# Reordering the start of a tile, and moving the place where TensorE's loop body ends, in a fused attention and FFN kernel

## The chip, the cores and the metric

One core of one Trainium2 chip. The time is device microseconds of one execution of the whole program. Median, lowest and highest are those of the runs shown; one further execution was recorded by the hardware profiler, and every row below comes from it.

## What is computed

A transformer layer over x of 4096 rows and 512 columns, float32, without a batch dimension to speak of:

```python
qkv = x @ w_qkv.T                       # 16 heads of 32, q, k, v
q, k = rope(q), rope(k)
scores = q @ k.T * scale                # a row sees itself and the 63 rows before it
out = softmax(scores) @ v @ w_out.T
x = layernorm(x + out)
gate = silu((x @ w_gate) * s_gate)      # 512 to 2048, int8 weights
up = (x @ w_up) * s_up
x = layernorm(x + ((gate * up) @ w_down) * s_down)
```

## The kernel before, in words

The rows are cut into 8 tiles of 512 (TILE), each of 4 blocks of 128 (NB = 4). Attention of tile a runs together with the FFN of tile a - 1: the 16 steps of a tile (STEPS) hold one gate product and one up product of the FFN each, and between them one group of four heads of one block of attention: scores, maxima, exponentials, weights (probabilities), their transpose by DMA, and the product with the values (weigh_v). Values and projections are float32; numbers that go into a float16 product are split into a high and a low half (split_high on ScalarE, split_low on GpSimd, split_v and split_x1 on VectorE).

Each engine has its program written out by hand, in order, with semaphores between them; nothing is planned by a tool. Each program has a first part, then a loop (Fori) over tiles whose body is back(t) followed by front(t + 1), then the last tiles. Tile 1 has a front of its own (is_early); the front that the diff touches runs for tiles 2 to 7.

- **TensorE** (from line 1035). back ends with project_pair (queries and keys) and begin_values. front begins with project_values: two row pairs (i = 0, 1), each of seven products of 128x256 called first, fifth, sixth, third, seventh, second, fourth (the values are made with seven products instead of eight, so several write one place of a bank one after the other, and each such product waits until ScalarE has copied the one before out, keep_values_...). Among them stand scores(0) and scores(1). Then the steps: gate s, up s, and after odd steps two weigh_v and two scores. weigh_v(0) and weigh_v(1) stand behind up 3, scores(5) and scores(6) behind them. The front ends with the output projection and the down blocks 0 and 1; back begins with spread_maximum (a small product that spreads the next tile's largest input) and the down blocks 2 and 3. So the loop body of TensorE ends between down blocks 1 and 2.
- **ScalarE** (from line 1506). Copies of the products, split_high(2) and split_high(3) (four parts each: two of the queries, two of the keys, of blocks 2 and 3), exponentials(0), keep_v (high half of the values), exponentials(1), then per step a tanh, copies and exponentials.
- **VectorE** (from line 2093). add_v (finishes the values of a block), maxima and bias of a group, weights, split_v; then per step two operations of swiglu, maxima, bias, weights. GpSimd's and VectorE's sums of a tile's inputs lie in ffn_tmp and probs, where later the FFN's and attention's values go.
- **GpSimd** (split_low, line 797). split_low(1), (2), (3) in this order, four subtractions each (L800), every one behind the part of split_high that it needs; then per step split_probs (L690) and split_fuse (L695).
- **SyncE**, which issues the DMAs in order. turn_qk(0), (1), (2) transpose queries and keys of a block and each wait until split_low of that block is done (qk_low); behind them cross_v(0), cross_v(1) (four DMAs L571), turn_probs(0) (a transpose, L587), cross_v(2), turn_probs(1), cross_v(3), and so on. weigh_v(1) waits for turn_probs(1) to have landed. The order is:

```python
for j in range(1, NB - 1):
    turn_qk(a, j)
for j in range(2):
    cross_v(a, j)
for s in range(STEPS):
    turn_probs(a, s, ffn)
    if s < 2:
        cross_v(a, NB - 2 + s)
```

## Time and profile before

| | |
|---|---|
| runs: median, lowest, highest | 1166.68 us, 1164.76, 1167.25 |
| profiled execution, its own time | 1166.12 us |
| its span, first to last instruction | 1164.3 us |
| TensorE busy | 1148.5 us, 99% |
| VectorE, ScalarE, GpSimd busy | 84%, 53%, 52% |
| granted TensorE clock | 0.998 of full speed |

The time of the profiled execution is its span and 1.8 us around it. Busy is the share of the span in which the engine had an instruction under way; the ends of matmuls are modelled, so two that follow each other without a stall overlap in the rows, and the distance from start to start tells more than the duration.

### The profile page before, as it was taken

The numbers are of one execution on the slowest core, as the hardware profiler recorded it, in microseconds if no ns is written. First come the engines' busy times: TensorE is split into PE (matmuls) and PEld (weight loads), VectorE is DVE, ScalarE is ACT, GpSimd is POOL, SyncE is SP. The second block draws the span as 40 slices with busy tenths as digits, with TensorE's granted clock in tenths as the row PEclk, the third lists the DMA queues.
The fourth block names the chain that finished last, engine by engine and source line by source line (L and its number), as shares of the span: only waits on it lengthen the run. The fifth ranks groups of instructions, "written<-read, shape, count | busy, mean of one in ns | idle before, by whom it ended". The sixth has DMA issues, their size and how long they took to land.

```text
span 1164.3 us, 25889 instructions
## 1 busy us (share of the span) xinstructions
PE 1148.5 (99%) x8577; PEld 595.0 (51%) x8577; DVE 976.0 (84%) x2797; ACT 622.3 (53%) x1724; POOL 600.5 (52%) x570
## 2 busy tenths in 40 slices
PE   9999999999999999999999999999999999999998
PEld 4344446464464644646455464554645545464444
DVE  7889998889997899878999789887898978986434
ACT  3863883159920689117980279702796038950330
POOL 0775684356731667326771367614676245752330
PEclk9999999999999999999999999999999999999999
DMA  9999786357672585717757077561874627644000
GB/s 295 161 186 242 140 172 147 85 100 139 121 174 56 96 139 112 175 40 124 138 98 166 37 142 127 97 160 38 151 123 91 166 58 136 126 74 109 19 1 37
DMA packets 353042, 139.59 MB, mean 120 GB/s; under 512 B 309968, under 2 KB 332624, under 8 KB 352912
## 3 DMA queue, kind: packets, MB, share of 16 engines
q1 hardware_dynamic: 334976, 106.86, 49.6%
q0 software_dynamic: 10800, 18.09, 5.3%
q10 hardware_dynamic: 7136, 12.93, 3.2%
q8 instruction: 78, 1.28, 0.5%
q14 instruction: 52, 0.43, 0.1%
HBM read 36.13 MB, written 9.18 MB: 39 GB/s over the span
## 4 chain that ended last, share of the span: by engine, by line
PE 78%; DVE 7%; issue 6%; POOL 3%; DMA 3%; ACT 2%; SPq 1%; ACTq 0%; DVEq 0%; POOLq 0%
PE bank L906 52%; PE bank L1217 17%; PE bank L916 3%; PE bank L1143 2%; DMA xT_sb<-xT_sb 2%; DVE v_own L1794 2%; POOL xT_sb L690 1%; ACT bank L1457 1%; PE bank L1123 1%; ACT fuse L1356 1%; POOL fuse L695 1%; DVE ffn_tmp L1844 1%; DMA qkT<-fuse 1%; DVE bank L1831 1%; DVE probs L1809 1%
## 5 line engine op out<-in xcount | busy, mean ns | idle before, releaser
L906 PE MATMUL bank<-x1T,wg 128*128 128x512 f16 (+1 forms) x1032 | 242.5, 378 | 1.1 <-DVE ffn_tmp L1844 1.1
L906 PE MATMUL bank<-x1T,wu 128*128 128x512 f16 x1024 | 241.9, 379 | 0.0
L1457 ACT ACTIVATE bank<-bank,neg_max,qk_scale 128x128 f32<-128x128 f32 x512 | 220.4, 434 | 23.5 <-DVE neg_max L1837 22.4
L1217 PE MATMUL bank<-wd,fuse 128*128 128x512 f16 (+2 forms) x1056 | 223.3, 373 | 0.7 <-DVE y L1892 0.6
L695 POOL TENSOR_TENSOR fuse<-ffn_tmp,fuse 128x512 f16<-128x512 f32 x128 | 149.7, 1170 | 96.5 <-ACT fuse L1356 96.2
L800 POOL TENSOR_TENSOR fuse<-fuse 128x512 f16<-128x512 f32 x116 | 142.6, 1266 | 88.3 <-ACT fuse L1356 86.1
L1217 PEld LDWEIGHTS bank<-wd,fuse 128*128 128x128 f16 x1056 | 101.6, 98 | 118.7 <-DVE y L1892 1.6
L906 PEld LDWEIGHTS bank<-x1T,wu 128*128 128x128 f16 x1024 | 100.2, 98 | 120.6
L690 POOL TENSOR_TENSOR xT_sb<-probs,xT_sb 128x512 f16<-128x512 f32 x112 | 131.0, 1170 | 52.2 <-ACT xT_sb L1356 52.0
L906 PEld LDWEIGHTS bank<-x1T,wg 128*128 128x128 f16 x1032 | 96.4, 98 | 112.7 <-DVE ffn_tmp L1844 2.0
L1366 ACT ACTIVATE ffn_tmp<-bank,tanh_scale 128x512 f32<-128x512 f32 x128 | 88.7, 693 | 65.9 <-PE bank L906 42.2
L1831 DVE CUSTOM_DVE_ANT_0 bank<-bank,mask_tile 128x128 f32<-128x128 f32 x448 | 116.3, 321 | 7.6 <-issue 7.6
L1848 DVE SCALAR_TENSOR_TENSOR ffn_tmp<-bank,fuse_scale,ffn_tmp 128x512 f32<-128x512 f32 x128 | 96.1, 751 | 18.8 <-PE bank L906 6.6
L1844 DVE SCALAR_TENSOR_TENSOR ffn_tmp<-ffn_tmp,bank 128x512 f32<-128x512 f32 x128 | 86.8, 678 | 25.6 <-ACT ffn_tmp L1366 25.5
L1457 ACT ACTIVATION_READ_ACCUMULATOR bank<-bank,neg_max,qk_scale 128x1 f32 x512 | 105.6, 206 | 0.0
L885 POOL TENSOR_TENSOR rstd<-mean_var,half_power 128x1 f32<-128x1 f32 x32 | 24.0, 751 | 144.1 <-DVE mean_var L1865 138.6
L1356 ACT ACTIVATE fuse<-bank 128x512 f32<-128x512 f32 x24 | 14.3, 597 | 140.7 <-PE bank L906 138.8
L1356 ACT ACTIVATE fuse<-ffn_tmp 128x512 f16<-128x512 f32 x128 | 80.7, 630 | 16.1 <-DVE ffn_tmp L1848 16.1
L1809 DVE SCALAR_TENSOR_TENSOR probs<-bank,inv_sum 128x512 f32<-128x512 f32 x120 | 82.9, 691 | 4.8 <-DVE inv_sum L1804 0.3
L1356 ACT ACTIVATE fuse<-fuse 128x512 f16<-128x512 f32 x120 | 65.5, 619 | 36.4 <-DVE fuse L1635 36.4
L1627 DVE TENSOR_TENSOR fuse<-bank,tables 128x512 f32<-128x512 f32 x120 | 75.5, 681 | 3.8 <-POOL fuse L800 3.1
L815 POOL TENSOR_TENSOR rstd<-mean_var,half_power 128x1 f32<-128x1 f32 x32 | 23.8, 745 | 98.4 <-DVE mean_var L1865 98.4
(258 smaller groups left out, 1846.7 us busy)
## 6 DMA issues: line engine op xcount, KB each, us to landing
v_cross<-v_own SPq DMA_DIRECT2D x64, 128.0 KB, 2.4
out<-x ACTq DMA_DIRECT2D x31, 256.0 KB, 2.0
xT_sb<-xT SPq DMA_DIRECT2D x30, 256.0 KB, 4.9
qkT<-x SPq DMA_DIRECT2D x28, 256.0 KB, 3.2
wg<-w_gate POOLq DMA_DIRECT2D x7, 1024.0 KB, 5.7
v_cross<-kept_v_weights ACTq DMA_DIRECT2D x5, 768.0 KB, 7.5
wu<-w_up POOLq DMA_DIRECT2D x7, 512.0 KB, 6.3
wqkv<-w_qkvT SPq DMA_DIRECT2D x8, 256.0 KB, 6.2
```

The lines of the kernel that those rows point to most:

```text
L690: done(probs_low, pool.tensor_tensor(place[:, 1, :, :], probs_place(s, ffn), place[:, 0, :, :], ALU.subtract))
L695: done(fuse_low, pool.tensor_tensor(fuse[:, s, 1, :], ffn_tmp[:, s % 2, :], fuse[:, s, 0, :], ALU.subtract))
L800: last = pool.tensor_tensor(*low_operands(j, i, ffn), ALU.subtract)
L906: last = pe.matmul(dst, lhsT, rhs, start=(i == 0 and not onto), stop=(i == len(pairs) - 1), skip_group_check=onto)
L1217: last = pe.matmul(dst[:, cols], fuse[:, s, z, rows], wd[:, s, cols], start=(s == 0 and z == 0), stop=(s == STEPS - 1 and z == 1))
L1356: return act.activation(dst, src, ACT.Copy, scale=scale)
L1366: done(tanh_done, act.activation(ffn_tmp[:, s % 2, :], bank32[2 * (s % 2)], ACT.Tanh, scale=tanh_scale[:, s:s + 1]))
L1457: last = act.activation(unit, unit, ACT.Exp, bias=neg_max[:, s % 2, h // 3, h % 3:h % 3 + 1], scale=qk_scale[:, 2:3], accum_out=row_sum[:, ...
L1809: done(probs_ready, dve.scalar_tensor_tensor(out=probs_place(s, ffn), in0=units, scalar=2.0 ** PROB_BITS, in1=inverse, op0=ALU.mult, op1=A ...
L1831: last = dve.tensor_tensor_reduce(out=unit, in0=unit, in1=mask_tile[:, :], scale=1.0, scalar=MASKED, op0=ALU.add, op1=ALU.max, accum_out=r ...
L1844: done(gated, dve.scalar_tensor_tensor(out=tmp, in0=tmp, scalar=1.0, in1=bank32[2 * (s % 2)], op0=ALU.add, op1=ALU.mult))
L1848: done(fused, dve.scalar_tensor_tensor(out=tmp, in0=bank32[2 * (s % 2) + 1], scalar=fuse_scale[:, s:s + 1], in1=tmp, op0=ALU.mult, op1=ALU ...
```

## The change

The order on three engines changes at the start of the fronts of tiles 2 to 7. On TensorE the second product of pair 0 comes earlier, and scores(0) and scores(1) come before sixth, fourth, third and seventh of what is left. On ScalarE the key half of split_high(2) and all of split_high(3) move behind copies and exponentials. On VectorE maxima and bias of groups 0 and 1 come before add_v(1), and the split_v are spread between others, with one more wait: weights(0) overwrites probs, which seventh(1) reads. The programs of GpSimd and SyncE are as before. Apart from that, TensorE's loop body ends behind down block 2 instead of behind down block 1; the order of its products there stays down 0, down 1, spread_maximum, down 2, down 3.

```diff
-        V_FIRST, V_FIFTH, V_SIXTH, V_THIRD, V_SEVENTH, V_SECOND, V_FOURTH = range(7)
+        V_FIRST, V_FIFTH, V_SIXTH, V_THIRD, V_FOURTH = 0, 1, 2, 3, 6
+        V_SECOND, V_SEVENTH = (4, 5), (5, 4)
...
             def project_values(a):
                 values_sixth(a, 0)
                 values_third(a, 0)
+                values_second(a, 0)
                 values_fifth(a, 1)
                 values_seventh(a, 0)
+                scores(a, 0, True)
+                scores(a, 1, True)
                 values_sixth(a, 1)
-                values_second(a, 0)
                 values_fourth(a, 0)
                 values_third(a, 1)
                 values_seventh(a, 1)
-                scores(a, 0, True)
-                scores(a, 1, True)
                 values_second(a, 1)
                 values_fourth(a, 1)
...
-                for j in range(2):
+                for j in range(NB - 1):
                     down(f, j, attn)
+                    if more and j == 1:
+                        spread_maximum(a)
 
             def back(t, more, attn=True):
                 a, f = t, t - 1
-                if more:
-                    spread_maximum(a)
-                for j in range(2, NB):
-                    down(f, j, attn)
+                down(f, NB - 1, attn)
...
                     keep_values_sixth(a, 0)
                     keep_values_fifth(a, 1)
                     keep_values_seventh(a, 0)
+                    split_high(a, 2, ffn, range(2))
                     keep_values_sixth(a, 1)
-                    split_high(a, 2, ffn)
+                    exponentials(a, 0, ffn)
                     keep_values_seventh(a, 1)
-                    split_high(a, 3, ffn)
-                    exponentials(a, 0, ffn)
                     keep_v(a, 0, ffn)
                     keep_v(a, 1, ffn)
+                    split_high(a, 2, ffn, range(2, 4))
                     exponentials(a, 1, ffn)
+                    split_high(a, 3, ffn)
                     keep_v(a, 2, ffn)
                     keep_v(a, NB - 1, ffn)
...
                     add_v(a, 0)
-                    add_v(a, 1)
                     for s in range(2):
                         maxima(a, s, ffn)
                         bias(a, s)
-                        add_v(a, 2 + s)
+                    add_v(a, 1)
+                    wait(v_product[1], dve, a - 2, V_SEVENTH[1])
                     weights(a, 0, ffn)
-                    for j in range(2):
-                        split_v(a, j, ffn)
+                    add_v(a, 2)
+                    split_v(a, 0, ffn)
+                    add_v(a, NB - 1)
+                    split_v(a, 1, ffn)
                     weights(a, 1, ffn)
                     for j in range(2, NB):
                         split_v(a, j, ffn)
```

## Rows read from the trace of the kernel before

**Rows 1.** The page, busy time of each engine

```profile
PE 1148.5 (99%) x8577; PEld 595.0 (51%) x8577; DVE 976.0 (84%) x2797; ACT 622.3 (53%) x1724; POOL 600.5 (52%) x570
```

**Rows 2.** TensorE's waits from 200 us on: total, times, longest

```profile
PE bank L1143 <- DMA xT_sb<-xT_sb: 2.0, 4, 0.6
PE bank L906 <- DVE ffn_tmp L1844: 1.1, 6, 0.2
PE bank L1196 <- issue: 0.8, 1, 0.8
PE bank L1217 <- DVE y L1892: 0.6, 1, 0.6
```

**Rows 3.** Timeline of TensorE in tile 3: start, duration, instructions

```profile
400.78 0.52 PE L1123 MATMUL bank<-qkT 128*32 128x96 f16 x32
401.23 1.13 PE L906 MATMUL bank<-wqkv,xT_sb 128*128 128x256 f32 x4
...
411.14 1.90 PE L906 MATMUL bank<-x1T,wg 128*128 128x512 f16 x8 [0.17 <-DVE ffn_tmp L1844]
...
418.39 0.28 PE L1143 MATMUL bank<-xT_sb,v_cross 128*32 128x128 f16 x8
...
418.61 0.84 PE L1123 MATMUL bank<-qkT 128*32 128x96 f16 x32
419.38 1.90 PE L906 MATMUL bank<-x1T,wg 128*128 128x512 f16 x8
```

**Rows 4.** Timeline of ScalarE at the start of tile 3

```profile
397.80 2.18 ACT L1356 ACTIVATE fuse<-fuse 128x512 f16<-128x512 f32 x4
400.88 0.47 ACT L1356 ACTIVATE v_cross<-bank,v_scale 128x256 f32<-128x256 f32 x1 [0.90 <-PE bank L906]
...
408.90 0.71 ACT L1366 ACTIVATE ffn_tmp<-bank,tanh_scale 128x512 f32<-128x512 f32 x1
```

**Rows 5.** The page, costliest groups: one exponential

```profile
L1457 ACT ACTIVATE bank<-bank,neg_max,qk_scale 128x128 f32<-128x128 f32 x512 | 220.4, 434 | 23.5 <-DVE neg_max L1837 22.4
```

**Rows 6.** Timeline of GpSimd, split_low(2) and (3) of tile 3

```profile
398.50 9.43 POOL L800 TENSOR_TENSOR fuse<-fuse 128x512 f16<-128x512 f32 x8 [6.81 <-ACT fuse L1356]
```

**Rows 7.** Instructions of line 800, tile 3: duration ns min, median, max

```profile
L800 POOL TENSOR_TENSOR fuse<-fuse x8: 1156/1161/1610, 398.5 to 406.3; 128x512 f16<-128x512 f32 x8
```

**Rows 8.** Timeline of VectorE in tile 3

```profile
406.84 1.64 DVE L1794 TENSOR_TENSOR v_own<-ffn_tmp,v_own 128x512 f16<-128x512 f32 x1
...
410.41 0.68 DVE L1844 SCALAR_TENSOR_TENSOR ffn_tmp<-ffn_tmp,bank 128x512 f32<-128x512 f32 x1
```

**Rows 9.** Timeline of SyncE's issues in tile 3

```profile
403.12 4.55 SPq L541 DMA_TRANSPOSE qkT<-fuse  x2
...
407.95 2.52 SPq L571 DMA_DIRECT2D v_cross<-v_own  x4
...
411.61 2.03 SPq L587 DMA_TRANSPOSE xT_sb<-xT_sb  x1
...
415.25 1.24 SPq L587 DMA_TRANSPOSE xT_sb<-xT_sb  x1
```

**Rows 10.** Timeline of SyncE's issues in tile 1

```profile
126.11 2.51 SPq L571 DMA_DIRECT2D v_cross<-v_own  x4
...
131.63 1.25 SPq L587 DMA_TRANSPOSE xT_sb<-xT_sb  x1
```

**Rows 11.** Timeline of TensorE in tile 7, the weigh_v behind step 3

```profile
987.29 0.30 PE L1143 MATMUL bank<-xT_sb,v_cross 128*32 128x128 f16 x8 [0.45 <-DMA xT_sb<-xT_sb]
```

**Rows 12.** Timeline of TensorE at a loop end

```profile
635.29 0.23 PE L1196 MATMUL bank<-unit_rows,next_max 128*128 128x128 bf16 x1
```

**Rows 13.** Windows before the old and the new loop end: busy, clock, DMA share, GB/s

```profile
348.40:352.00 3.60, 3.60 (x19) 1.57 (x17) 3.37 (x6) 0.63 (x1) 0.00 (x0) 1.00 0.59 113
355.30:358.90 3.60, 3.60 (x19) 1.60 (x18) 3.29 (x16) 0.00 (x0) 0.00 (x0) 1.00 0.02 5
```

**Rows 14.** Timeline of GpSimd before a late loop end

```profile
772.27 0.74 POOL L794 DMA_DIRECT2D wu<-w_up  x1 [6.88 <-issue]
```

More of the change, by code:

```diff
@@ L1408, in keep_values_seventh @@
             def keep_values_seventh(a, i):
-                keep_value_product(a, i, v_rows(2 * i + 1)[:, 0:HALF_EMB], v_places(i)[3], V_SEVENTH)
+                keep_value_product(a, i, v_rows(2 * i + 1)[:, 0:HALF_EMB], v_places(i)[3], V_SEVENTH[i])
             def carry_v(a):
@@ L1786, in add_v @@
                 wait(v_products_kept[i], dve, a - 2, 2 + back)
-                wait(v_product[i], dve, a - 2, V_FOURTH if back else V_SECOND)
+                wait(v_product[i], dve, a - 2, V_FOURTH if back else V_SECOND[i])
                 done(v_added, dve.scalar_tensor_tensor(out=v_rows(j), in0=bank32[j], scalar=v_scale[:, 1:2],
```

## The prediction

> **What bounds the kernel.** I read the page first: TensorE is busy for 1148.5 of the 1164.3 us [rows 1], so the change can win only stalls of TensorE, and anything it adds to TensorE's path is paid in full. Next come TensorE's waits from 200 us on, behind the odd first tiles: four kinds, 4.5 us together [rows 2]. Two belong to the front and its consequences: the third gate product waits for VectorE's first swiglu operation in each of the six tiles, and four weigh_v wait for a transposed block of probabilities. The view leaves out the start-up of a stall: the 32 score matmuls take 0.45 us from start to start where nothing waits (400.78 to 401.23), 0.77 us behind weigh_v(1) in tile 3 (418.61 to 419.38) [rows 3], where scores(6) waits for weights(3) of VectorE. Last I read the queues that feed weigh_v(1): ScalarE to GpSimd (L800) to SyncE to the DMA. There the point of the change lies. In tile 3 turn_probs(1) is issued at 415.25 [rows 9] and weigh_v(1) starts at 418.39 [rows 3], without a wait: at most 3.14 us from issue to use. In tile 7 the same product already waits 0.45 us [rows 11]. So there is next to no slack on this path.
>
> **TensorE's values and scores.** The same products in another order; nothing is added, and the number of changes between scores and values is the same. In tile 3, scores(0) and (1) move from 400.78 by four 128x256 products of about 0.86 us to about 397.3, sixth(1) to 397.8, seventh(1) to 400.5, and the first gate product stays where it is. ScalarE's copy of seventh(1) began 1.07 us behind its product's start, so it moves from 400.88 [rows 4] to about 401.54 and lasts 0.47; fourth(1), which waits for it, still begins at 402.2. Slack 0.2 us: cost nothing, at worst 0.1 us per tile.
>
> **ScalarE.** The same work again. The query half of split_high(2) starts at 397.80 as before; copies of 128x512 follow each other in 0.52 us (2.18 us for four) [rows 4]. Then sixth(1) is copied at 398.95 to 399.3, exponentials(0) take 4 x 0.434 = 1.74 us [rows 5] to 401.1, the engine idles to 401.54 for seventh(1), then keep_v(0) and (1) to 402.95. Only then come the two key parts of split_high(2), 402.95 to 404.0, exponentials(1) to 405.7, split_high(3) to 407.8, two keep_v to 408.85, and the first tanh: 408.85 against 408.90 before [rows 4]. ScalarE gains nothing for the FFN; VectorE does, for split_v(2) and (3) now lie right behind the copies instead of behind weights(1): its first swiglu operation moves from 410.41 [rows 8] to about 409.65. A lead of 0.75 us takes away the wait of the third gate product and of scores(6). The added wait of weights(0) for seventh(1), done at 401.5, holds VectorE's add_v(2) and split_v(0) for 0.4 us, in time that it had to spare before exponentials(1).
>
> **GpSimd and SyncE, whose programs do not change.** This is the cost. Before, split_low(2) began at 398.50, 0.70 us behind its first part [rows 4, 6], and eight subtractions took 9.43 us with one of 1.61: the seven others 1.12 apart, so the fourth ended at 402.97 and SyncE issued the transposes of block 2 at 403.12 [rows 6, 7, 9]. Now its third part can start at 402.95 + 0.70 = 403.65 and the fourth ends at 405.9: 2.9 us later. SyncE works in order, and behind that pair stand cross_v(0) and (1), turn_probs(0), cross_v(2), turn_probs(1). From the pair's issue to the first cross_v it takes 4.83 us [rows 9]; from there to turn_probs(1), when nothing but SyncE itself is waited for, 5.52 us (tile 1, 126.11 to 131.63) [rows 10]. That gives 403.12 + 2.9 + 4.83 + 5.52 = 416.4 instead of 415.25, and weigh_v(1) at 416.4 + 3.1 = 419.5 instead of 418.39: **1.1 us more** per tile. The slack between cross_v and turn_probs(0) (1.1 us idle, and the latter's 2.03 us against 1.24) [rows 9] is already used up in this sum. Split_low(3) ends near 408.1 + 3.1 = 411.2, still ahead of turn_probs(0), which SyncE now reaches at 413.6.
>
> **A collision that may lengthen it.** One split_v lasted 1.64 us beside L800 instead of 0.68, and one L800 1.61 instead of 1.16 [rows 7, 8]. In the new order split_v(0) and (1) fall on the two key parts. Bounds: nothing, or 0.45 us more per tile; no row decides, and I take the middle, 0.2. The Trainium skill (SBUF — State Buffer, in its text on the shared port pair) says that a VectorE operation with two SBUF inputs and a GpSimd operation that reads SBUF exclude each other for the whole instruction. By that rule the upper end would hold and the total below would be 1.5 us higher; the trace agrees as far as the lengths of these two instructions go.
>
> **The sum over six tiles.** Tiles 2 to 6 lose 1.3 us each, tile 7, which waits 0.45 us there already (0.6 with the stall's start-up), about 0.7: +7.2. Behind this stall TensorE is about 1 us later, so other stalls vanish: scores(6) in five tiles, 0.32 us each less what one of them lacks, -1.5; the weigh_v of step 7 in three tiles, 2.0 - 0.45 = 1.55 us [rows 2, 11] with 0.17 us start-up for each, -2.1. The wait of the third gate product goes too, but it lies ahead of weigh_v(1), which starts at an absolute time: it brings nothing. Total of the front: **+3.6 us**.
>
> **The loop end.** spread_maximum began at 635.29 [rows 12], 0.26 us late behind a loop end; at another end the wait was 0.8 us with nothing in the profile that ended it [rows 2], but there the next product had to wait for VectorE anyway. DMA engines are 0.59 busy in the stretch ahead of the old end and 0.02 in that 7 us later [rows 13]. I take -0.3 us; the bounds are 0 and -1.1. The page Runtime: NRT & Kernel Launch of the Trainium skill (Instruction fetch mechanics) says a taken branch breaks the sequential prefetch and makes the target be fetched by a DMA. By it a quiet DMA stretch shortens the branch, which supports the -0.3; if the fetch has a fixed cost instead, the sum would be 0.3 higher.
>
> Against the profiled execution's own 1166.12 us this makes 1166.12 + 3.6 - 0.3 = **1169.4 us**; that execution lies 0.6 us below the median of the runs shown, within their spread.
>
> **Rivals.**
> - *Slower as worked out*, 1167 to 1172: 46 in 100. For it: SyncE's order, and a stall that tile 7 already shows.
> - *Faster, because SyncE's chain is not the last* (26). It decides if turn_probs(1) is issued by 415.25 despite the push, that is if the key parts come no more than 1.8 us later (1.1 idle and 0.75 in turn_probs(0)'s longer issue), or if the pair of transposes is issued 1 us faster. Then weigh_v(1) follows the earlier weights, and all stalls go: six gate waits of 0.24 = 1.4, scores 1.5, step 7 2.1, tile 7 0.6, loop 0.3: 5.9 us, 1160.2. Half of it is 1163. Against it: 2.9 us is fixed by seventh(1) and two copies.
> - *No change* (18): the stall is 1.1 us or less and the one stray event of the old trace, a GpSimd DMA issue held for 6.88 us [rows 14] that made that tile about 2 us longer, does not come back: 1166.12 + 2 - 2 = 1166.
> - *Slower by more* (10): turn_probs(0) or (1) keeps an issue of 2.03 us although SyncE comes straight from cross_v: +0.75 us per tile, 1174; both, 1178.
>
> **Numbers.** About 0.2% (2.3 us) is what a measurement of this kernel can tell from no change, so slower starts at 1169.0. The main case spreads over that line: of its 46 some 8 fall within 0.2%, the last rival adds 10 to slower: 0.48. The range has to take in half and most of the faster case and one slow issue per tile: 1161.5 to 1175.
>
> **What would show it.** Right: L541 for block 2 issued about 3 us later after the first gate product; SyncE going from cross_v straight to turn_probs(0) and (1); a wait of about 1 us of L1143 for a DMA behind step 3 in each of tiles 2 to 7; no wait of L906 for L1844. Wrong: turn_probs(1) issued at the old distance from the first gate product; L1143 waits as few as before; new waits of the values' fourth product for ScalarE; a longer spread_maximum gap at the new loop end.

## The result, and the profile after

The changed kernel takes **1186.32 us** (median; 1183.64 to 1188.15), beside 1165.92 us (1164.76 to 1167.25) for the kernel before on the same chip: a ratio of 1.0173, with a 95% interval of 1.0149 to 1.0196. It is slower, as forecast, but by 20 us and not by 3. The profiled execution took 1185.87 us with a span of 1184.0 us, 19.75 us more than the one shown of before, and it is this difference that is taken apart here.

The page of the changed kernel, busy time of each engine (of before: [rows 1]):

```profile
PE 1150.9 (97%) x8577; PEld 595.2 (50%) x8577; DVE 981.1 (83%) x2797; ACT 622.9 (53%) x1724; POOL 604.8 (51%) x570
```

The same 8577 matmuls are busy for 2.4 us more (some ran at a lower clock, below), while the span grew by 19.7. The time is in stalls. TensorE's waits in the changed kernel from 200 us on (total, times, longest):

```profile
PE bank L1144 <- DMA xT_sb<-xT_sb: 11.2, 7, 2.3
PE bank L1218 <- issue: 7.6, 4, 2.3
PE bank L907 <- DVE ffn_tmp L1845: 3.1, 6, 0.5
```

Against [rows 2]: the wait of weigh_v for a transposed block grew from 2.0 to 11.2 us, the wait of the third gate product from 1.1 to 3.1 us instead of going away, and a kind that was not there stands at the down products (L1218), four times, with nothing in the profile that ends it. Measured from start to start of the matmuls, which takes in the start-up of each stall, the difference is: loop ends +9.7 us, weigh_v(1) +11.6, third gate product +2.0, and -3.5 for stalls of scores(6) and of step 7's weigh_v that went. That is 19.8 of the 19.75 us.

**The front.** TensorE in tile 3, timeline of the changed kernel (start, duration, instructions, idle time before and what ended it; lines are one further down than in [rows 3]):

```profile
408.89 1.89 PE L907 MATMUL bank<-x1T,wg 128*128 128x512 f16 x8
...
417.32 1.90 PE L907 MATMUL bank<-x1T,wg 128*128 128x512 f16 x8 [0.51 <-DVE ffn_tmp L1845]
...
426.39 0.29 PE L1144 MATMUL bank<-xT_sb,v_cross 128*32 128x128 f16 x8 [1.65 <-DMA xT_sb<-xT_sb]
```

From here on G is the start of the first gate product of a tile: 403.06 us in tile 3 before, 408.89 after. weigh_v(1)'s waiting product starts at G + 17.50 instead of G + 15.33. Behind it stand the queues. ScalarE in the same tile, timeline of the changed kernel (of before: [rows 4]):

```profile
408.78 1.14 ACT L1356 ACTIVATE fuse<-fuse 128x512 f16<-128x512 f32 x2
...
414.68 0.69 ACT L1366 ACTIVATE ffn_tmp<-bank,tanh_scale 128x512 f32<-128x512 f32 x1
```

GpSimd in the same tile and view (of before: [rows 6]):

```profile
404.33 2.28 POOL L801 TENSOR_TENSOR fuse<-fuse 128x512 f16<-128x512 f32 x2 [6.81 <-ACT fuse L1356]
409.47 8.21 POOL L801 TENSOR_TENSOR fuse<-fuse 128x512 f16<-128x512 f32 x6 [2.87 <-ACT fuse L1356]
```

SyncE's issues, likewise (of before: [rows 9]):

```profile
412.31 4.66 SPq L542 DMA_TRANSPOSE qkT<-fuse  x2
417.25 2.85 SPq L572 DMA_DIRECT2D v_cross<-v_own  x4
420.44 1.24 SPq L588 DMA_TRANSPOSE xT_sb<-xT_sb  x1
...
423.28 1.23 SPq L588 DMA_TRANSPOSE xT_sb<-xT_sb  x1
```

ScalarE splits the keys at 408.78. GpSimd, which before did eight subtractions in a row, does two, stands still for 2.87 us, and does six; the fourth ends at 412.2. SyncE issues the pair of transposes at G + 3.42 (before G + 0.06), and from there to turn_probs(1) at G + 14.39 (before G + 12.19) its issues follow each other almost without a pause. The block lands 3.1 us later, and weigh_v(1) starts.

VectorE in tile 3, timeline of the changed kernel (of before: [rows 8]):

```profile
414.30 0.80 DVE L1795 TENSOR_TENSOR v_own<-y,v_own 128x512 f16<-128x512 f32 x1 [1.69 <-ACT v_own L1356]
415.02 1.65 DVE L1795 TENSOR_TENSOR v_own<-v_cross,v_own 128x512 f16<-128x512 f32 x1
416.58 0.68 DVE L1845 SCALAR_TENSOR_TENSOR ffn_tmp<-ffn_tmp,bank 128x512 f32<-128x512 f32 x1
```

VectorE has been idle for 1.69 us, and then split_v(3) lasts 1.65 us, beside GpSimd's subtractions. The first swiglu operation starts at G + 7.69 instead of G + 7.35: later, not earlier.

**The loop end.** TensorE's timeline around the second loop end of the changed kernel (of before: [rows 12]):

```profile
503.82 5.29 PE L1218 MATMUL bank<-wd,fuse 128*128 128x512 f16 x23
511.15 5.10 PE L1218 MATMUL bank<-wd,fuse 128*128 128x512 f16 x15 [2.05 <-issue]
```

The window behind the stall (busy time of PE, PEld, DVE, ACT, POOL, then granted clock, DMA share, GB/s, as in [rows 13]):

```profile
511.20:514.60 3.40, 3.40 (x9) 1.24 (x10) 0.62 (x3) 0.00 (x0) 1.34 (x2) 0.52 0.24 84
```

In the middle of a run of the same kind a down product starts late: at 364.31, 511.15, 658.00 and 802.88 us, by 2.50, 2.21, 1.69 and 1.80 us. That is once per round of the loop, each time behind the fourth product of the new body. Behind the first two of these stalls the clock granted to TensorE is about half (0.52 in this window, so 1.2 instead of 2.4 GHz for nearly all of its 3.4 us), after TensorE had stood still for over 2 us; 7 or 8 products then take 0.43 us each in place of 0.216, 1.7 us more.

### The profile page after: what moved, and what is told of

It is laid out like the page before. It is cut to its first block, busy times and chain, and to the rows that moved or that the text cites. A ratio compares the mean times of both kernels' runs of the same rounds, so it can differ in the third digit from the quotient of the medians.

```text
span 1184.0 us, 25906 instructions
## 1 busy us (share of the span) xinstructions
PE 1150.9 (97%) x8577; PEld 595.2 (50%) x8577; DVE 981.1 (83%) x2797; ACT 622.9 (53%) x1724; POOL 604.8 (51%) x570
## 4 chain that ended last, share of the span: by engine, by line
PE 70%; issue 11%; POOL 6%; SPq 5%; DVE 4%; DMA 3%; ACT 1%; POOLq 0%; ACTq 0%; DVEq 0%
PE bank L907 43%; PE bank L1218 18%; POOL fuse L801 5%; PE bank L1144 3%; SPq L542 2%; DMA xT_sb<-xT_sb 2%; SPq L572 2%; PE bank L917 2%; PE bank L1124 1%; PE bank L933 1%; DVE fuse L1628 1%; DMA out<-x 1%; SPq L588 1%; PE bank L1240 1%; ACT bank L1457 1%
## 5 line engine op out<-in xcount | busy, mean ns | idle before, releaser
L1218 PE MATMUL bank<-wd,fuse 128*128 128x512 f16 (+2 forms) x1056 | 227.1, 376 | 7.6 <-issue 7.6
L801 POOL TENSOR_TENSOR fuse<-fuse 128x512 f16<-128x512 f32 x116 | 148.6, 1310 | 105.9 <-ACT fuse L1356 103.5
L1218 PEld LDWEIGHTS bank<-wd,fuse 128*128 128x128 f16 x1056 | 102.1, 99 | 129.7 <-issue 15.1
L886 POOL TENSOR_TENSOR rstd<-mean_var,half_power 128x1 f32<-128x1 f32 x32 | 24.0, 750 | 154.6 <-DVE mean_var L1866 149.1
L1356 ACT ACTIVATE xT_sb<-probs 128x512 f16<-128x512 f32 x112 | 70.6, 631 | 8.2 <-DMA xT_sb<-xT_sb 8.1
```

The source lines that it names most:

```text
L801: last = pool.tensor_tensor(*low_operands(j, i, ffn), ALU.subtract)
L1218: last = pe.matmul(dst[:, cols], fuse[:, s, z, rows], wd[:, s, cols], start=(s == 0 and z == 0), stop=(s == STEPS - 1 and z == 1))
L1356: return act.activation(dst, src, ACT.Copy, scale=scale)
```

## The experiments

Fifteen kernels in four groups, each group on one chip beside the kernel before.

**First group: which half of the change costs what, and is it the place of the loop body?** TensorE's whole instruction stream was counted in the built programs: ahead of the loop's body stand 3447 instructions in the kernel before and 3514 in the changed one (a float16 product counts as 2, its weight load and itself; a float32 product as 4). The bodies are equally long. The traces agree: 2224 instructions stand between two branches in every kernel, and 67 more ahead of the first branch in the changed one. Theory A: a position of the body's start is bad, whatever the order of the work. Theory B: the new loop end itself is bad.

loop_alone is the kernel before with the change's loop end:

```diff
-                for j in range(2):
+                for j in range(NB - 1):
                     down(f, j, attn)
+                    if more and j == 1:
+                        spread_maximum(a)
```

> The kernel before with TensorE's loop end behind down block 2 and nothing else. Theory: the loop end costs by itself, and the front has no part in it. Adding up the stalls of TensorE in the two traces, the four loop ends cost about 12 us in the changed kernel and 2 in the one before, so I expect +8 to +10 us against before (about 1175), a stall of 1.7 to 2.5 us a few products behind each of four loop ends, and the granted clock at half behind some of them. Rival: the stall comes from TensorE being late through the new front; then this kernel is within 2 us of before.

Measured: 1176.71 us (1175.85 to 1180.75) beside 1165.59, ratio 1.0109 [1.0086, 1.0132]. The one kind of its waits that grew beyond a microsecond or so, in that view (L1143's wait for a DMA went from 2.0 to 3.3 us):

```profile
PE bank L1217 <- issue: 8.4, 4, 2.3
```

The loop end alone brings the four stalls and costs 11 us, one more than the 8 to 10 expected.

front_alone is the changed kernel with the old loop end (the diff above, reversed).

> The changed kernel with TensorE's loop end back behind down block 1. Theory: the front costs what the delayed chain through SyncE costs: +10 us against before (about 1176), with weigh_v(1) waiting 1.6 to 2.2 us for its transposed block in each of tiles 2 to 7, no stall at loop ends over 0.5 us, and the clock at full speed. Rival (front and loop end act together): the sum of this kernel's and loop_alone's differences is more than 3 us away from the 20 us of the whole change.

Measured: 1176.15 us (1175.62 to 1176.59), ratio 1.0093 [1.0076, 1.011]. Its waits:

```profile
PE bank L1144 <- DMA xT_sb<-xT_sb: 11.4, 7, 2.2
PE bank L907 <- DVE ffn_tmp L1846: 3.1, 6, 0.5
PE bank L1197 <- issue: 1.6, 2, 1.1
```

The front alone costs 10.6 us, and 11.1 + 10.6 = 21.7 is within 1.3 us of the 20.4 us of both: the two halves very nearly add. One part of the expectation missed: with the old loop end a wait for issue of 1.1 us stands at spread_maximum (L1197), where none over 0.5 was expected. This is the small stall of [rows 2] (0.8 us at L1196) again; more on it below.

The other two shift the body by waits that have long been met, at each step of TensorE's first down blocks, ahead of the loop. new_end_shifted has the new loop end and two such waits per step of block 0, which the built program has as one instruction, 16 in all: its body starts at 3530. old_end_shifted has the old loop end and five per step of blocks 0 and 1, 68 instructions: 3515.

```diff
+                        if isinstance(f, int) and f == 0 and j in (0,):
+                            for _ in range(2):
+                                pe.wait_ge(wd_in, 4 * 16)
                         for z in range(2):
```

> The kernel before, loop end where it was, but 68 instructions (waits that are met at once) put into TensorE's program ahead of the loop, in the first down blocks, so that the loop body begins at the same place of the instruction stream, to one instruction, as in the changed kernel. Theory A, what counts is where the body's first instruction lies in the stream: stalls of about 2 us a few products behind each loop end, +8 to +10 us against before. Theory B, what counts is which products stand behind the loop end or what the DMA engines do at that time: within 1 us of before, no stall over 0.5 us.

> loop_alone, with 16 instructions (waits that are met at once) put into TensorE's program ahead of the loop, so that the body begins 16 instructions later in the stream than in the changed kernel. In its trace the stall came about 10 instructions behind the body's first. Theory A, place in the stream: the stall is gone, the time is that of before within 1.5 us. Theory B, the place of the loop end among the products: as loop_alone, +8 to +10 us.

Measured: old_end_shifted 1179.34 us (1177.34 to 1181.23), ratio 1.0114 [1.0092, 1.0136]; new_end_shifted 1162.15 us (1161.13 to 1163.38), ratio **0.9972 [0.9961, 0.9983]**. TensorE's waits for issue in old_end_shifted, in the same view as above:

```profile
PE bank L1220 <- issue: 12.0, 4, 3.1
PE bank L1196 <- issue: 1.7, 3, 1.1
```

(Three lines of 0.2 to 1.1 us are left out.) Its timeline behind a loop end, with spread_maximum and one down product of the new body done:

```profile
500.85 15.21 PE L1220 MATMUL bank<-wd,fuse 128*128 128x512 f16 x63 [2.94 <-issue]
```

And the waits of new_end_shifted (one line more, of 0.3 us, is left out):

```profile
PE bank L906 <- DVE ffn_tmp L1846: 1.1, 6, 0.2
PE bank L1143 <- DMA xT_sb<-xT_sb: 0.6, 1, 0.6
```

That settles A against B. The old loop end, moved to where the change had put the body, stalls as the new one does; the new one, 16 instructions further on, has no wait for issue in the view, and the kernel is 3.4 us faster than before. Both sizes missed, though not the side: old_end_shifted costs 13.8 us instead of 8 to 10, for its four stalls are longer (3.0 to 3.3 us), and new_end_shifted was expected within 1.5 us of before.

**Second group: the front.** Theory Q is the prediction's: the late key parts hold turn_qk(2), and SyncE hands the delay on, in order. Theory G: VectorE and GpSimd are late with the probabilities themselves. All four start from front_alone or from one another. keys_ahead lets ScalarE split all of block 2 early; sync_reordered leaves ScalarE alone and moves one issue of SyncE:

```diff
-                    split_high(a, 2, ffn, range(2))
+                    split_high(a, 2, ffn)
                     keep_values_sixth(a, 1)
...
-                    split_high(a, 2, ffn, range(2, 4))
```

The edit of sync_reordered, in SyncE's program:

```diff
-                    for j in range(1, NB - 1):
-                        turn_qk(a, j)
+                    turn_qk(a, 1)
                     for j in range(2):
                         cross_v(a, j)
+                    turn_qk(a, 2)
```

> This kernel has the new front and the old loop end (as front_alone, 1176.15 us, where TensorE waited 11.4 us in 7 stalls of 2.2 us for the second half of the transposed probabilities at L1144), and ScalarE makes all four high parts of score block 2 before it keeps the sixth products of the second half. Theory Q (the weigh_v wait is handed on through SyncE's fixed order: the late low part of block 2 holds turn_qk(2), and turn_qk(2) holds everything SyncE issues behind it): GpSimd's low parts of block 2 end about as early as in the kernel before, turn_qk(2) is issued at the first gate product of the tile instead of 3.4 us behind it, and the wait at the second weigh_v falls from 2.2 us to about 0.5 us a tile. ScalarE keeps the sixth and the seventh products about 0.5 us later, for which TensorE should wait at values_fourth(1), some 0.35 us a tile. In all 6 to 8 us less than front_alone: 1168 to 1170 us. Theory G (the probabilities are late because VectorE's and GpSimd's own work on them is late, and SyncE's order has nothing to do with it): the wait at the second weigh_v stays at 2 us or more, and the time stays at 1175 to 1178 us.

> This kernel is front_alone (1176.15 us) with one issue of SyncE moved: turn_qk(2) is issued behind cross_v(0) and cross_v(1) instead of ahead of them. No engine's own work is touched. Theory Q: cross_v(0) is no longer held until 3.4 us behind the first gate product, turn_probs(0) follows as soon as GpSimd's probabilities of block 0 are there (9.9 us behind the first gate product instead of 11.5), turn_probs(1) at about 12.5 instead of 14.4, and the second weigh_v waits 0.2 to 0.5 us a tile instead of 2.2: about 10 us less than front_alone, 1165 to 1167 us. The wait of the third gate product (0.58 us in six tiles) stays. Theory G: turn_probs(1) is issued when VectorE and GpSimd are done with block 1, which this edit doesn't change: 1175 to 1178 us. A third outcome: turn_qk(2) is now late for whoever reads the turned keys of block 2; then a new wait stands at the scores of block 2.

Measured: keys_ahead 1166.9 us (1164.37 to 1168.45), ratio 1.0005 [0.9995, 1.0015]; sync_reordered 1170.51 us (1169.38 to 1170.9), ratio 1.0036 [1.0021, 1.005]. The waits of keys_ahead from 200 us on (one more, for issue at L1197, 1.2 us in two, is left out):

```profile
PE bank L1144 <- DMA xT_sb<-xT_sb: 2.8, 7, 0.6
```

SyncE's issues in tile 3 of keys_ahead, G = 406.56:

```profile
406.18 4.53 SPq L542 DMA_TRANSPOSE qkT<-fuse  x2
...
415.57 1.94 SPq L588 DMA_TRANSPOSE xT_sb<-xT_sb  x1
...
419.11 1.24 SPq L588 DMA_TRANSPOSE xT_sb<-xT_sb  x1
```

The waits of sync_reordered (left out again: for issue at L1197, 0.9 us):

```profile
PE bank L1144 <- DMA xT_sb<-xT_sb: 5.5, 10, 1.1
PE bank L907 <- DVE ffn_tmp L1846: 3.1, 6, 0.5
```

SyncE's issues in tile 3 of sync_reordered, G = 405.15:

```profile
405.91 2.67 SPq L572 DMA_DIRECT2D v_cross<-v_own  x4
409.00 4.38 SPq L542 DMA_TRANSPOSE qkT<-fuse  x2
415.16 1.84 SPq L588 DMA_TRANSPOSE xT_sb<-xT_sb  x1
...
418.60 1.23 SPq L588 DMA_TRANSPOSE xT_sb<-xT_sb  x1
```

Q holds. With the keys early, turn_qk(2) is issued at G - 0.38 and turn_probs(1) at G + 12.55, close to the G + 12.19 of before. With only SyncE's order changed and every engine's own work as in front_alone, turn_probs(1) comes at G + 13.45 in place of 14.39, and the kernel wins 5.6 us. It was forecast to win 10: turn_probs(0) came at G + 10.0 as expected, but turn_probs(1) was 0.9 us later than the 12.5 expected. That turn_probs(0) was 1.84 us under issue and not 1.24 makes 0.6 of it, and half of the wait at L1144 stayed (5.5 of 11.4 us). In keys_ahead the feared wait for ScalarE's copies did not come, and the gate products' waits for VectorE went altogether (its first swiglu operation started at 413.25, G + 6.69), which was not forecast: it is about what it won beyond the 6 to 8 us (9.3 us).

values_later is sync_reordered with two splits of VectorE moved, and both_mended adds to it the new loop end and 16 instructions, start at 3530:

```diff
                     weights(a, 1, ffn)
-                    for j in range(2, NB):
-                        split_v(a, j, ffn)
...
+                    if s == 1 and attn and not is_early(a):
+                        for j in range(2, NB):
+                            split_v(a, j, ffn)
```

> This kernel is sync_reordered with VectorE's splits of the last two value blocks moved behind its first swiglu. Theory V (the wait of the third gate product is VectorE's first swiglu, which ends later because the splits ahead of it run beside GpSimd's work at 1.60 to 1.65 us in place of 1.16 or 0.80): the first swiglu starts at least 1.5 us earlier than 7.7 us behind the first gate product, and the 6 waits of 0.5 us at the third gate product go: about 3 us less than sync_reordered, 1162 to 1164 us. Rival: that wait isn't VectorE's but ScalarE's tanh (5.8 us behind the first gate product in both kernels); then the six waits stay and the time is that of sync_reordered. What can go wrong: the last two blocks of split values come later for cross_v(2) and cross_v(3), and the third weigh_v waits instead.

> This kernel is values_later with the new loop end, and with 16 instructions more on TensorE ahead of the loop, so that the body of the loop starts 3530 instructions into TensorE's stream, where the kernel with the new loop end alone and shifted so (1162.15 us, ratio 0.9972) had no stall behind its four loop branches. Theory A (the stall behind a loop branch comes of where the body lies in the stream, not of the new loop end): no stall over 0.3 us behind any of the four branches, the granted clock stays at full speed, and the gain of the mended front adds to that of the shifted end: 1157 to 1161 us, faster than the kernel before. Rival: the new loop end leaves too little queued work when the front's waits are gone, and the four stalls of 1.7 to 2.5 us are back with about 10 us: 1170 us.

Measured: values_later 1178.57 us (1177.83 to 1179.57), ratio 1.0108 [1.0091, 1.0125]; both_mended 1176.94 us (1176.61 to 1177.51), ratio 1.0097 [1.008, 1.0114]. Both expectations missed. The waits of values_later that grew:

```profile
PE bank L907 <- DVE ffn_tmp L1846: 9.5, 6, 1.6
PE bank L1124 <- DVE probs L1811: 5.2, 6, 0.9
```

VectorE in tile 3 of values_later, G = 405.80, timeline:

```profile
413.78 1.58 DVE L1796 TENSOR_TENSOR v_own<-y,v_own 128x512 f16<-128x512 f32 x1
415.29 1.64 DVE L1796 TENSOR_TENSOR v_own<-v_cross,v_own 128x512 f16<-128x512 f32 x1
...
418.12 0.68 DVE L1846 SCALAR_TENSOR_TENSOR ffn_tmp<-ffn_tmp,bank 128x512 f32<-128x512 f32 x1
```

Of theory V the direction holds: the first swiglu operation came at G + 6.5 (412.31), 1.2 us sooner, and the third gate product no longer waited. But now both splits ran at 1.58 and 1.64 us, in front of the maxima and the second swiglu operation, and the fourth gate product waited 1.6 us, the scores 0.9. The 3.1 us of splits only changed the product that waits for them. both_mended has no wait for issue at its loop ends (its view has none, and from start to start no product behind a branch is more than 0.23 us late), so the part of its expectation on them holds; the rest fell with values_later.

**Third group: the position again, and a best version.** after_shifted is the changed kernel itself plus the 16 instructions (3530). new_end_later is the kernel before with the new loop end and 256 of them, 16 at each step (3770, which is 3514 + 256).

> This is the changed kernel itself (1186.32 us) with 16 waits more, already met, in TensorE's instructions ahead of the loop, so that the loop's body starts 3530 instructions into its stream instead of 3514. The work and its order are those of the changed kernel. Theory A (where the body lies decides the stall behind the branch): the four stalls of 1.7 to 2.5 us and the half clock behind two of them go, a round of the loop falls from 144.5 to 147.5 us to about 143 us, and the time is that of the new front alone, 1174 to 1177 us. Rival B (the new loop end leaves too little queued work at the branch once the new front changes what comes ahead of it): the stalls stay, 1184 to 1188 us.

> This is the kernel before with the new loop end, as in new_end_shifted (1162.15 us), but with 256 met waits ahead of the loop instead of 16: the body starts 3770 instructions into the stream, 256 behind the 3514 at which loop_alone stalled (1176.71 us, rounds of 145.5, 143.7 and 144.1 us against 141.0 us with the body at 3530). Theory A in its sharper form (instructions come in blocks of 256, and it is the place within a block that counts): the stalls are back, four of 1.7 to 2.5 us a few weight loads behind the branch, the rounds last 143.5 to 145.5 us, and the time is 1174 to 1178 us plus what the waits themselves cost (up to 5 us). Its weaker form (any body that starts further on is fine, or the waits themselves are what helps): no stall, rounds of 141.0 us, 1162 us plus the cost of the waits.

Measured: after_shifted 1177.24 us (1175.78 to 1180.33), ratio 1.0092 [1.0076, 1.0109]; new_end_later 1199.59 us (1195.87 to 1200.88), ratio 1.0278 [1.0258, 1.0298]. TensorE's waits in after_shifted (there is one kind more, 3.1 us at the third gate product, as in the changed kernel):

```profile
PE bank L1144 <- DMA xT_sb<-xT_sb: 13.1, 7, 2.1
```

The largest of new_end_later's waits:

```profile
PE bank L1220 <- issue: 19.8, 19, 2.1
```

Its timeline at the first loop end:

```profile
386.38 1.93 PE L1220 MATMUL bank<-wd,fuse 128*128 128x512 f16 x5 [1.97 <-issue]
```

With nothing changed but 16 met waits, the changed kernel loses the four stalls and 9.1 us (8.75 when each is held against the kernel before on its own chip). And 256 instructions behind the first bad place lies another: stalls at 386.39, 531.89, 675.74 and 821.11 us, rounds of 145.5, 143.9 and 145.4 us, where new_end_shifted has 141. So it is the place within a stretch of 256 instructions that counts, not how far the body lies from the start. The total of new_end_later overshot because the waits cost far more than the 5 us allowed: where 16 waits stand between two pairs of products, the pairs start 1.73 to 1.87 us apart in place of 0.43 (15 of the 19 waits in the view), and the granted clock from 200 to 300 us averaged 0.86. One such instruction is 0.105 us behind the one before it: one per pair of products, as in new_end_shifted, is covered by the pair's 0.43 us, and 16 are not.

keys_end is keys_ahead with the new loop end and the 16 instructions; keys_sync_end has turn_qk(2) behind cross_v(1) as well.

> This is keys_ahead (1166.9 us: the new front with all of ScalarE's high parts of block 2 ahead of the last copies, old loop end) with the new loop end and the 16 instructions that put the body at 3530. If the gain of the shifted new end (3.6 us against the kernel before, in new_end_shifted) adds to this front as it did to the old one, the time is 1162 to 1164 us, no better than new_end_shifted (1162.15 us), and the repaired front brings nothing. If the waits of 0.4 us at the second weigh_v in 7 tiles are partly those of rounds that the branch had delayed, it falls to 1159 to 1161 us.

> This is keys_end with turn_qk(2) issued behind cross_v(1) as well. By theory Q turn_probs(0) is bound by GpSimd's probabilities at 8.9 us behind the first gate product in either order, so that this brings at most 0.2 us a tile: 0 to 1.5 us less than keys_end. If the wait at the second weigh_v (2.8 us in 7 tiles in keys_ahead) comes of SyncE's chain still, it goes and the time is 2.5 us less.

Measured: keys_end 1163.36 us (1161.97 to 1165.34), ratio 0.998 [0.9971, 0.999]; keys_sync_end 1167.31 us (1166.03 to 1170.46), ratio 1.0017 [1.0008, 1.0027]. The only kind of wait that keys_end has left from 200 us on:

```profile
PE bank L1144 <- DMA xT_sb<-xT_sb: 1.6, 3, 0.9
```

SyncE's issues in tile 3 of keys_sync_end, G = 404.13:

```profile
405.13 2.43 SPq L572 DMA_DIRECT2D v_cross<-v_own  x4
407.99 5.75 SPq L542 DMA_TRANSPOSE qkT<-fuse  x2
414.09 1.23 SPq L588 DMA_TRANSPOSE xT_sb<-xT_sb  x1
```

The gain of the shifted loop end adds to this front (3.5 us), and with its keys split early the front of the change is worth nothing: 1163.36 us is not better than the 1162.15 of new_end_shifted, which has the old front and beats both kernels. keys_sync_end missed: it was to gain 0 to 1.5 us and lost 4. The pair of transposes, issued right behind the four copies, took 5.75 us in place of the 4.60 of keys_end, ended at G + 9.6, and turn_probs(0) was bound by it and not by GpSimd (G + 9.96; in keys_end G + 9.01). The place behind the copies is not what makes the pair long: it stands there in sync_reordered and values_later too and takes 4.1 to 4.6 us in tiles 2 to 6. In the same tiles of keys_sync_end and both_mended, which have the new loop end, it takes 5.5 to 6.1 us. What links the two is open.

**Fourth group: where the border lies, and what the new loop end is worth without it.** Three positions more: the new loop end at 3520 and at 3528, and the old one at 3531 (two waits per step in 6 and in 14 steps; six per step in 28 steps).

> The kernel before with the new loop end, its body starting 3520 instructions into TensorE's stream (loop_alone: 3514, 1176.71 us; new_end_shifted: 3530, 1162.15 us). Theory A with a border: in the changed kernel, which starts at 3514, the stalled product is some ten instructions into the body, so that the border lies near 3524. A body that starts at 3520 then meets it after 4 instructions, with fewer products under way to cover: four stalls at least as long as in loop_alone (2.1 to 2.4 us), perhaps 1 us longer, and nearer to the branch; 1176 to 1181 us. If the stall instead fades with the distance from 3514 (some other effect of the place, without a border), it is about half here: 1166 to 1172 us.

> The same with the body at 3528, a few instructions behind the supposed border near 3524. Theory A with that border: no stall behind the four branches, as at 3530, 1161 to 1164 us. If the border lies behind 3528, the stalls are there, 1176 us or more.

> The kernel before with its own loop end and 84 met waits as instructions in two down blocks ahead of the loop, so that its body starts at 3531 instead of 3447. Up to 3 instructions stand between two pairs of products, 0.105 us each by the trace of new_end_later, which is covered by the 0.43 us of the pair. If the place alone made new_end_shifted 3.4 us faster than before, this kernel gains as much: 1161 to 1164 us. If it is the order (spread_maximum and down 2 ahead of the branch), it stays at 1164.5 to 1167 us, the small stalls at L1196 with it.

Measured, beside 1166.78 us: new_end_3520 1180.68 us (1176.65 to 1183.42), ratio 1.0108 [1.008, 1.0136]; new_end_3528 1162.68 us (1161.08 to 1164.11), ratio 0.9969 [0.9959, 0.9978]; old_end_3531 1162.95 us (1161.5 to 1165.14), ratio **0.9962 [0.995, 0.9974]**. The largest of new_end_3520's waits:

```profile
PE bank L1220 <- issue: 11.0, 4, 2.8
```

Its timeline at the first and second loop end:

```profile
363.37 9.83 PE L1220 MATMUL bank<-wd,fuse 128*128 128x512 f16 x31 [2.82 <-issue]
510.75 6.87 PE L1220 MATMUL bank<-wd,fuse 128*128 128x512 f16 x31 [2.83 <-issue]
```

All waits of old_end_3531 from 200 us on:

```profile
PE bank L1143 <- DMA xT_sb<-xT_sb: 0.9, 2, 0.5
PE bank L906 <- DVE ffn_tmp L1847: 1.0, 6, 0.2
PE bank L1196 <- issue: 0.4, 2, 0.2
```

At 3520 the four stalls are 2.7 to 3.0 us from start to start, 2.9 on average against 2.3 in loop_alone; at 3528 there is no wait for issue. The stall stands behind the first product of the body at 3520 and behind the fourth at 3514 and 3770. With a weight load and a product for each that is the same place of the stream, 3520 + 2 = 3514 + 8, and 256 behind it. The effect doesn't fade with the distance, it grows up to a border between 3520 and 3528 and ends there. And the old loop end, moved to 3531, is as fast as the new one at 3528 or 3530: the new loop end by itself is worth nothing that the times can tell, and what made new_end_shifted faster than before was its place. Why 3531 is better than 3447, by 3.8 us, stays open in part: the granted clock is the same, the waits from 200 us on are 2.3 us in place of 4.5 [rows 2], and which of the rest comes from the place no run tells. The two rows of the timeline also show what the lower clock costs: the same 31 products behind stalls of one length, in 9.83 us and in 6.87.

**What the stall waits for.** The traces hold the fetches of instructions too, as DMA packets of 16384 bytes on queue 8. The pages of new_end_3520 and new_end_3528, line of that queue (packets, MB, share):

```profile
q8 instruction: 78, 1.28, 0.5%
q8 instruction: 74, 1.21, 0.4%
```

The packets are TensorE's: one of them starts 0.9 to 2.3 us behind the start of each of its 68 taken branches (17 kernels, four each). From one branch to the next there are 11 packets with the body at 3447, 3514, 3515, 3520 or 3770, and 10 with it at 3528, 3530 or 3531, for the same 2224 instructions: one border less. The first packet brings the start of the body; TensorE's branch, which is in the trace as well, ends 1.3 to 1.65 us behind its landing and lasts 3.3 to 4.7 us (0.08 us where it is not taken, at the end of the loop). The down products queued ahead of it cover up to about 3.8 us. The second packet starts only 0.65 to 1.65 us behind the end of the branch, and in all 20 long stalls (five kernels, four each) TensorE goes on 1.23 to 1.62 us behind its landing: in the changed kernel it landed at 362.70, 509.84, 656.72 and 801.48 us. Where the border is 37 products away, as at 3447, or 250 instructions, as at 3528, the second packet lands in time. The small stalls at spread_maximum are the branch itself, longer than the queued products: 0.9 us in the kernel before at 778.01 us, where the first packet started 1.92 us behind the branch and not 1.0, and the branch lasted 4.46 us.

## Why the prediction was right or wrong

**Right: the front's mechanism.** The prediction said that the push of the keys reaches weigh_v(1) through GpSimd and SyncE's order, and each step is there: the key parts at 408.78 - 408.89 = G - 0.1 (forecast 402.95, the same), the first tanh at G + 5.79 (G + 5.79), the low parts of block 2 at G + 3.3 (G + 2.8), turn_probs(1) at G + 14.39 (G + 13.3). The wait of L1144 for a DMA stands in each of tiles 2 to 7, and keys_ahead and sync_reordered show the cause by shrinking it in two ways, from 11.4 us to 2.8 and to 5.5. The stalls that were to vanish behind it did: -3.5 us, forecast -3.6.

**Mis-sized: "1.1 us more" and "I take the middle, 0.2".** Of 1.3 us forecast per tile 2.17 came. The collision took the upper end: low parts G + 3.3 in place of 2.8. For a VectorE operation with two SBUF inputs beside a reading GpSimd operation the Trainium skill (SBUF — State Buffer, on the shared port pair) had said just that, and its upper end was the better choice. The traces agree: a split lasts what is left of GpSimd's running instruction and 0.55 us more (0.80 us with 0.24 left, 0.98 with 0.44, 1.58 with 1.03, 1.64 with 1.09), and 0.68 alone. The other 0.6 us came from SyncE's own issues, which were summed at their shortest: from the pair to the first copy it took 4.94 us (forecast 4.83), and from there to turn_probs(1) 6.03 (5.52, from tile 1), of it the four copies 2.85 in place of 2.51. Over tiles 2 to 7 the term was forecast at 7.2 us and measured at 11.6.

**Wrong: "A lead of 0.75 us takes away the wait of the third gate product".** The first swiglu operation was to start at 409.65 - 403.06 = G + 6.6 and started at G + 7.69. Split_v(2) began at G + 5.4, where the forecast copies put it, but the two splits lasted 0.80 and 1.65 us and not 0.68 each: the collision, priced in one place, was forgotten in the other. The wait grew from 0.24 to 0.58 us, six times: 2.0 us. That it is VectorE's splits, values_later shows.

**Wrong: "I take -0.3 us; the bounds are 0 and -1.1".** This is the step that failed. The loop end cost 9.1 us (after_shifted), 10.2 (front_alone) or 11.1 us (loop_alone). A loss had been excluded with no row that excluded it: the bounds were taken from the stalls that the old end showed, at 0.8 us at most, as if these belonged to the loop end and not to where it lay. What the runs showed in its place: a stall of 1.7 to 3.3 us a few products into the body whenever the body starts at 3514, 3515, 3520 or 3770 instructions, and none of that kind with 3528, 3530 or 3531, with either loop end. At 3447 and 3531 there are only the small ones at spread_maximum, up to 1.2 us. Of the 16.4 us by which the profiled execution was missed, the loop ends make 10.0, weigh_v(1) 4.4 and the third gate product 2.0. The -0.3 had the right sign: at the first product behind the four branches the traces show 1.2 us lost in all in old_end_3531 and 0.06 in new_end_3528 (1.2 to 2.3 us in the kernels with the old end, 0.06 to 0.5 with the new), and the first packet starts up to 2.3 us behind the branch at the old end and up to 1.5 at the new. The medians, 1162.95 and 1162.68 us, are too close to tell. The change altered that place without meaning to, since moving a down block over the loop end puts 67 instructions more ahead of the body. The prediction had used a page of the Trainium skill (Runtime: NRT & Kernel Launch, Instruction fetch mechanics) for the gain alone. By the same section instructions are fetched in 16 KiB blocks of 256, the next one while the block before runs, and a taken branch to a target that isn't at hand makes it be fetched anew. The traces agree: packets of 16384 bytes, the same stall at 3514 and at 3770, a border between 3520 and 3528, and a fetch behind each taken branch. They also show what the forecast left out: the fetch of the next block starts only when the branch is over, and a body that starts ten instructions or fewer ahead of a border needs that block at once.

Of the rivals, "faster" needed turn_probs(1) at its old distance from the first gate product, which was missed by 2.2 us, and "no change" a stall of 1.1 us or less, where weigh_v(1) waited 1.65 us in tile 3; "slower by more" had the right side but the wrong mechanism: turn_probs(0) and (1) were issued in 1.24 us, so its price was never paid. The range ended at 1175; each half alone ended just above it.

## What to carry to other kernels

A change that adds or removes instructions ahead of a hardware loop moves the loop's body in its engine's stream, and here a shift of 8 to 84 instructions, with the same work, was worth 4 to 18 us over four loop ends: judge a reordering only after trying it at two or three positions of the body, with a few met waits ahead of the loop, look for waits put down to issue a few instructions behind the branch, and read the instruction packets around it. When work is pushed back on one engine, follow it through every in-order queue behind it and price both sides of every collision that it causes.

## What the hardware showed that was not expected

- The place of the loop's body: starts at 3514, 3515, 3520 and 3770 instructions stall for 1.7 to 3.3 us a few products behind each of four loop ends; 3447, 3528, 3530 and 3531 don't. The stall ends 1.23 to 1.62 us behind the landing of a 16384-byte instruction packet.
- A taken branch lasts 3.3 to 4.7 us on TensorE, and is hidden only behind products queued ahead of it.
- Whether the clock falls behind such a stall isn't settled by its length. In new_end_3520 it fell behind three stalls of 2.7 to 3.0 us and not behind one of 3.0; in the changed kernel behind 2.50 and 2.21 us and not behind 1.69 and 1.80. Where it fell, 6 to 14 down products took 0.43 us each in place of 0.216.
- A wait that is already met takes TensorE 0.105 us: nothing that shows when it stands alone between two pairs of products, while 16 stretch a pair from 0.43 to 1.73 - 1.87 us.
- SyncE's issue of a pair of transposes takes 4.4 to 4.7 us in tile 3 of most kernels here, but 5.75 in keys_sync_end and 5.68 in both_mended, and the cause is open; a single one takes 1.24 or up to 2.03 us [rows 9].
